# Two fused transformer layers on one core: five buffers of split weight chunks for four, twelve exponentials for fourteen

## The reference

```
xn = layernorm(x)
x  = x + attention_0(xn) + ffn_0(rmsnorm(xn) * ln_w)     # 32 heads of 16, 8 key/value groups, causal; ffn 1792 wide
xn = layernorm(x)
x  = x + attention_1(xn) + ffn_1(xn)                     # 32 heads of 16, causal, biases on q, k, v, out; ffn 1376 wide
attention: softmax(q k^T / 4, causal) v, then Wo
ffn:       (silu(x Wg) * (x Wu)) Wd
```

## Time and profile before

| | |
|---|---|
| runs | 811.23 us median of 3 (810.88 to 814.6) |
| the profiled execution | 813.03 us; span of the core 811.1 us |
| mean granted TensorE clock | 0.993 |
| busy: TensorE, VectorE, ScalarE, GpSimd | 769.3, 520.8, 406.4, 403.7 us |
| TensorE in the chain that ended last | 79% of the span |

### The profile page before, as it was taken

How to read it: one execution, slowest core, us unless ns; L and a number is a source line. 1 busy time by engine, 2 the same in 40 slices (tenths; PEclk the granted TensorE clock), 3 DMA queues, 4 the chain that set the end, 5 groups by cost and what they waited for, 6 DMA issues and landing times.

```text
span 811.1 us, 19165 instructions
## 1 busy us (share of the span) xinstructions
PE 769.3 (95%) x7172; PEld 589.6 (73%) x7172; DVE 520.8 (64%) x1536; ACT 406.4 (50%) x756; POOL 403.7 (50%) x549
## 2 busy tenths in 40 slices
PE   7899999999999999999979989997989989999996
PEld 4788888877777876687657767674766767787764
DVE  7777765677765678766578668515776857765323
ACT  2253455466655556545535564452364635645630
POOL 4344555555755554455435544357454644555631
PEclk9999999999999999999999999999899999999999
DMA  6557347463736363637784373289628586833331
GB/s 220 135 190 165 116 145 159 115 150 101 159 110 141 117 142 108 141 103 155 206 159 161 87 149 100 68 194 216 168 100 166 157 173 195 150 118 108 96 103 66
DMA packets 71932, 113.79 MB, mean 140 GB/s; under 512 B 21144, under 2 KB 21144, under 8 KB 71832
## 3 DMA queue, kind: packets, MB, share of 16 engines
q1 hardware_dynamic: 71840, 112.57, 55.3%
HBM read 87.04 MB, written 25.43 MB: 139 GB/s over the span
## 4 chain that ended last, share of the span: by engine, by line
PE 79%; DVE 7%; DMA 6%; SPq 4%; issue 2%; ACT 2%; POOL 0%; DVEq 0%; ACTq 0%
PE bank L1347 63%; PE bank L1491 6%; PE bank L1475 4%; PE bank L1457 4%; SPq L940 3%; DMA w_raw<-weights_in 2%; DVE bank L1292 2%; DMA k_op<-qk_scratch 1%; DMA m_scratch<-m_rows 1%; DMA q_op<-m_scratch 1%; DVE gate L1254 1%; DVE xt_lo L1221 1%; ACT gate L1099 1%; PE bank L1367 1%; DMA x<-x_in 1%
## 5 line engine op out<-in xcount | busy, mean ns | idle before, releaser
L1045 POOL TENSOR_TENSOR w_lo<-w_raw,w_hi 128x512 fp32r<-128x512 f32 x202 | 264.2, 1319 | 124.6 <-ACT w_hi L1087 122.0
L1292 DVE CUSTOM_DVE_ANT_0 bank<-bank,causal 128x128 f32<-128x128 f32 (+3 forms) x512 | 237.0, 520 | 76.1 <-PE bank L1457 75.3
L1067 POOL TENSOR_SCALAR_AFFINE_SELECT p<-p 128x256 f32<-128x256 f32 (+1 forms) x320 | 118.2, 370 | 256.5 <-ACT p L1080 248.9
L1080 ACT ACTIVATE p<-bank 128x512 f32<-128x512 f32 x320 | 173.6, 597 | 119.2 <-PE bank L1475 118.7
L1347 PE MATMUL bank<-xt_hi,w_hi 64*128 64x512 f32 x1008 | 206.0, 400 | 13.5 <-DVE h L1263 4.8
L1347 PE MATMUL bank<-xt_lo,w_hi 64*128 64x512 f32 x1008 | 201.6, 391 | 0.0
L1347 PE MATMUL bank<-xt_hi,w_lo 64*128 64x512 f32 x1008 | 201.3, 391 | 0.0
L1087 ACT ACTIVATE w_hi<-w_raw 128x512 fp32r<-128x512 f32 x202 | 120.8, 631 | 33.5 <-DMA w_raw<-weights_in 17.0
L1347 PEld LDWEIGHTS bank<-xt_hi,w_hi 64*128 64x128 f32 x1008 | 98.4, 187 | 38.8 <-DVE h L1263 6.2
L1347 PEld LDWEIGHTS bank<-xt_hi,w_lo 64*128 64x128 f32 x1008 | 98.3, 187 | 18.6
L1347 PE MATMUL bank<-w_hi,h_hi 64*128 64x512 f32 x528 | 108.8, 405 | 3.1 <-ACT p L1080 1.4
(11 more groups left out here) (74 smaller groups left out, 700.6 us busy)
## 6 DMA issues: line engine op xcount, KB each, us to landing
w_raw<-weights_in SPq DMA_DIRECT2D x202, 256.0 KB, 3.1
qk_scratch<-qk_parts SPq DMA_DIRECT2D x24, 512.0 KB, 3.6
q_op<-qk_scratch SPq DMA_DIRECT2D x96, 128.0 KB, 4.7
o_scratch<-o_t SPq DMA_DIRECT2D x32, 256.0 KB, 3.1
k_op<-qk_scratch SPq DMA_DIRECT2D x48, 128.0 KB, 7.7
context<-o_scratch SPq DMA_DIRECT2D x16, 256.0 KB
inverse<-r_scratch SPq DMA_DIRECT2D x16, 256.0 KB
k_op<-k_scratch SPq DMA_DIRECT2D x48, 64.0 KB, 5.2
```

Source lines behind the costliest of these rows:

```text
L1045: pool.tensor_tensor(w_lo[:, c % SPLIT, :], w_raw[:, c % RAW, :], w_hi[:, c % SPLIT, :].bitcast(F32), ALU.subtract).then_inc(split_done, 1)
L1067: pool.affine_select(out=view, in_=view, compare_op=ALU.is_ge, fill=0.0, base=0, pattern=[[0, n], [1, P]] if n == 2 else [[1, P]], channel ...
L1080: act.activation(p32[:, j % PRING, :], bank_of(g)[:, :], ACT.Exp, scale=SCALE).then_inc(exp_done, 1)
L1292: last = dve.tensor_tensor_reduce(out=bank[:, at:at + n], in0=bank[:, at:at + n], in1=causal[:, 512 - n:], scale=1.0, scalar=LOWEST, op0=A ...
```

## The change

`SPLIT` goes from 4 to 5: `w_hi` and `w_lo` get a fifth buffer of 128 x 512 each, and the planner and the waits use chunk c-5 in place of c-4. `PRING` goes from 14 to 12: `p32` loses two buffers of the same size, so that the sum of memory stays. No instruction is added or removed. The four numbers that follow from them in the planner (`chunk_ready`, `chunk`, `p_freed`, `trans`) change the order in which steps are placed on every engine.

```diff
-RAW, SPLIT, HSPLIT, PRING = 4, 4, 3, 14
+RAW, SPLIT, HSPLIT, PRING = 4, 5, 3, 12
```

## The result

The changed kernel is slower: 821.58 us median of 6 runs (817.5 to 822.15), against 813.42 us for the kernel before in 6 runs; the ratio is 1.0084, 95% interval 1.0059 to 1.0108. The forecast was no difference, 812 us in 804 to 820.

The account below looks back on a forecast made before the run. TensorE, busy 769.3 of 811.1 us, was taken as the bound. Terms -0.3 - 0.5 + 0.5 + 1.0 = +0.7 us gave 811.9, called 812 us (no difference), from 811.23; range 804 to 820.

Parts of the forecast that it names:

- The redrawn order: Planner's placing of steps on all engines: new sizes shift all later choices; +1.0 us, bounds -7.7 and +8.
- quiet stretches: TensorE outside 390 to 670 us: only 3.7 us idle in 400 us, so a new order can hardly win there.
- PV has its own due place and stays: Step in the ring term (+0.5 us): PV does not move, so most boundaries are not emptied by moved T visits.
- The fifth buffer: Split chunks: one wlo taken from behind the bias additions may shorten a stall; -0.3 us, bounds 0 and -1.2.
- The loads: SyncE's queue: every other weight load can be issued one job earlier; -0.5 us, bounds -3.4 and +3.4.
- The second rival: ScalarE: earlier whi awaits late loads, delaying exponentials and PV; 820 us; slower by over 4 us, this or other bad luck: 0.32.
- The first rival: Stall after second value product and its half-rate clock go; 804 us; faster by over 4 us, this or other luck: 0.23.
- The ring's swaps: TensorE: 16 second T visits move behind PV, 9 of them to a later boundary; +0.5 us, bounds 0 and +3.1.
- All three signs of being wrong: Clock falls at another place, the 3.93 us gap is gone, or new L1491 waits for exponentials appear.
- The clock: TensorE's clock halved after idleness: 2.7 us within the first rival's 7.9 us, and 2.7 us extra in the second rival.
- ScalarE's waits for used chunks: Sign: ScalarE's 16.5 us of waiting for TensorE to be done with chunks should fall to about half.
- the stretch 90 to 390 us: Sign: TensorE's idleness in this stretch, 3.4 us in the kernel before, should stay under 6 us.

Follow-up runs that it names:

- order_y_14: Kernel before (four split buffers, ring of fourteen) with the planner taking an S or T visit as 0.27 us, not 0.25: ratio 1.0084 to the kernel before.
- order_x_14: Kernel before with the planner taking attention outputs' write and read as 4.5 and 8.5 us, not 4.0 and 8.0: ratio 1.0287 to the kernel before.
- split5_alone: Kernel before with five split buffers, ring still fourteen, order redrawn, tile xn moved to free memory: ratio 0.9979 to the kernel before.
- before_outputs_first: Kernel before with two SyncE steps exchanged, outputs of octet 6 read ahead of maxima of group 15: ratio 1.0087 to the kernel before.
- after_maxima_first: Changed kernel with one SyncE step moved, maxima of group 15 read ahead of outputs of octet 6: ratio 1.0005 to the kernel before.
- twelve_in_old_order: Four split buffers, ring of twelve, TensorE order of the kernel before except 16 T visits put behind PV: ratio 1.0136 to the kernel before.
- order_of_before_split5: Five split buffers in memory, ring of fourteen, xn moved, the kernel before's order on every engine: ratio 0.9997 to the kernel before.
- after_loads_first: after_maxima_first with two weight loads moved on SyncE's queue ahead of six key transfers and the bias load: ratio 1.0032 to the kernel before.
- after_kept_warm: Changed kernel plus 48 matmuls that compute nothing, placed in its three longest TensorE gaps: ratio 1.0026 to the kernel before.
- both_in_old_order: Five split buffers, ring of twelve, TensorE order of the kernel before except 16 T visits moved behind PV: ratio 1.0064 to the kernel before.
- xn_moved_only: Control: kernel before (four split buffers, ring of fourteen) with only the tile xn placed as in split5_alone: ratio 0.9994 to the kernel before.

## Why the prediction was wrong

**The step that failed** is "The redrawn order", sized at +1.0 us with bounds -7.7 and +8. Redraws at unchanged sizes measured +7 us and +23 us (order_y_14 and order_x_14, 0.84% and 2.87% of 814.8). The third redraw with fourteen exponentials, split5_alone, measured -2 us. The changed kernel lost 7 us (0.84%), and the sum had +0.7. The term deserved a bound far wider to the slow side. I had the right reason, that quiet stretches can only lose, and took an eighth of the 8 us that I had set as its bound. Three draws do not say what its middle should have been.

**What carried it** is one exchange on SyncE's queue, which I did not look for. The prediction said of the ring: "What can be late next is the end of the exponentials of group u+1". It did not name PV's own train (output write, output read), which moves forward with PV and stands on the queue that also brings the next group's maxima; "PV has its own due place and stays" was the step that hid it. That the exchange is enough for a loss of this size is shown by before_outputs_first, and that undoing it takes back most of the loss by after_maxima_first. That it is the only way in which a ring of twelve can lose is not so: twelve_in_old_order loses elsewhere.

**The fifth buffer**: -0.3 us taken, bounds 0 and -1.2. In the old order it is 0 within 0.3% (order_of_before_split5), as forecast. Beside a ring of twelve the programs with it are faster by more than my bound, 0.7 and 1.1% (1.0136 to 1.0064, 1.0194 to 1.0084), though how much of that is order is not shown. The profile names one wait for a split, of 1.3 us; it stands before an S visit, which uses no weights, and the kernel before has the same 1.32 us put down to VectorE, so I do not count it against the forecast.

**The loads**: -0.5 taken, bounds 3.4 either way. ScalarE's waits for raw loads went from 17.0 to 40.4 us. PV 21 lost 5.6 us and then 2.1 at half rate, in place of the 3.4 us before: 2.2 us more of waiting, inside the bound, and 4.3 with the half rate, outside it. The second rival's mechanism occurred, once and not three times, so that the time came out near its 820 us is chance. Its own price in the whole is not shown, as its removal moved the stall (after_loads_first), and split5_alone has the same 40 us of such waits without a loss.

**The first rival** came true in part: the stall of 3.93 us is down to 1.04 and half of its half rate is gone. The time gained there was lost elsewhere, and the prediction did not reckon with a rival of each kind in one run. All three signs of being wrong that it named did appear: half rate at other places, the 3.93 us gap gone, and a new wait of PV (L1491).

**The ring's swaps**: +0.5 taken, bounds 0 and +3.1. All 16 moved, as forecast. Their own price was never isolated, because no order changes by them alone: even twelve_in_old_order had the other engines placed anew.

**The clock** stood in the prediction only as a rider of the rivals. It is most of the change's loss: busy time, forecast within 3 us of 769, rose by 7.3. Over the runs of the kernel before itself, 24 on the chip of after_kept_warm, time falls by 0.7 us for each 0.001 of granted clock. A mean clock of 0.982 against 0.989 is thus, by estimate, about 5 us of 8. From one program to another the clock alone does not give the time: split5_alone has 0.985 and is not slower than before, both_in_old_order has 0.988 and is 0.6% slower.

**Right**: no second T visit stands before its PV any more, ScalarE's waits for used chunks were to fall to about half (16.5 to 9.4 us), and the end of the chain stayed TensorE's. **Wrong**, by a little: the stretch 90 to 390 us was to idle under 6 us and idled 7.7.

Still open is whether a smaller ring costs anything in a fair draw of orders. The spread of these ten programs, 3%, hides anything under 1%.

## What to carry to other kernels

When sizes feed a planner that writes the order, the change is a new order first and new sizes second. Price the redraw by what neighbours of the old order cost, and replay the old choices to see what the sizes do without it. Read the single DMA queue as a program of its own: ask of each wait on it what stands behind, above all where a wait for a landing is followed by something that TensorE needs next. And judge idle time by its longest pieces; the sum hardly moved here while the time did.

## What the hardware showed that I had not expected

Two traces of programs with the same order have gaps that differ by one or two tenths of a microsecond, and only one has half rate behind them. Before T visit 16.0 the kernel before idled 2.88 us, and xn_moved_only 3.02; only the second has half-rate time behind it (3.4 us by windows of 1 us). At PV 25 it was 2.82 and 3.00 us, again only the second, where the PV took 4.04 us in place of 2.35 (first the kernel before, then xn_moved_only):

```profile
662.06 2.35 PE L1491 MATMUL bank<-p,v_op 128*17 128x512 f32 x32 [2.82 <-ACT p L1080]
```

```profile
662.26 4.04 PE L1497 MATMUL bank<-p,v_op 128*17 128x512 f32 x32 [3.00 <-ACT p L1084]
```

But order_of_before_split5 idled 2.76 us there and did lose clock behind it, so the length of the gap alone does not decide. After a gap of 1.99 us near 30 us, too, the trace of before has half rate and that of split5_alone has none. With that goes the spread of the runs of one kernel: those of before on one chip lie over 1.3% (805.92 to 816.25 us), with the clock at 0.997 in the fastest and 0.987 to 0.988 in most of the slowest.

The write of 256 KB that followed twelve transfers of queries and keys took 9.87 us to land, and 8.6 us at the same place in the kernel before, where the median of the 32 such writes is 3.0 us.
